# A state-space layer whose output product is moved from VectorE and GpSimd to TensorE transposes, ScalarE and one VectorE sum

## The reference, cut to what matters

```python
dt = softplus(einsum(x_dbl[..., :64], Wdt) + bdt)          # per token and channel
Bm, Cm = x_dbl[..., 64:80], x_dbl[..., 80:96]              # per token and state
dA  = exp(dt[..., None] * A)
dBx = (dt * x)[..., None] * Bm[:, :, None, :]
def step(hc, inp):                                         # over the tokens of a sequence
    dA_t, dBx_t, C_t = inp
    hc = dA_t * hc + dBx_t
    return (hc, einsum('bdn,bn->bd', hc, C_t))
y = (ys + x * Dp) * silu(z);  out = einsum('bld,ed->ble', y, W_out)
```

## Time and profile before

| what | value |
|---|---|
| median of 3 executions | 4015.16 us (4012.3 to 4021.78) |
| profiled execution, device time | 4010.37 us |
| its span, first to last instruction | 4008.4 us |
| mean granted TensorE clock | 0.933 of full speed |
| busy: PE / VectorE (DVE) / ScalarE (ACT) / GpSimd (POOL) | 87% / 68% / 48% / 39% |
| `recur`, first scan to last | 2884.9 to 3811.1 us after the start |

### The profile page before, as it was taken

The page is one execution under the profiler, slowest core; times in us unless marked ns, Lnnn a source line. Parts: engine busy times, 40 slices in busy tenths (PEclk is TensorE's granted clock), DMA queues, the critical chain, the costliest instruction groups (busy, mean ns, idle before and its releaser), DMA issues. The chain is left out here.

```text
span 4008.4 us, 128424 instructions
## 1 busy us (share of the span) xinstructions
PE 3504.0 (87%) x53914; PEld 2508.5 (63%) x53915; DVE 2740.8 (68%) x4691; ACT 1943.7 (48%) x3015; POOL 1561.9 (39%) x1491
## 2 busy tenths in 40 slices
PE   6999999999782899579999999998778788788778
PEld 4888888888671566348888888884232333333257
DVE  5777777777442122257777777776799999999964
ACT  2666666666441122126666666664444444444432
POOL 3333333333132000333333333330278877778900
PEclk8999999999895899879999999999898999999989
DMA  2010010010006100111001001000123222222200
GB/s 68 28 36 28 28 36 28 29 36 12 10 1 263 35 29 31 56 47 36 28 28 36 28 28 36 28 12 25 35 72 85 67 69 71 70 71 78 74 23 21
DMA packets 79949, 182.70 MB, mean 46 GB/s; under 512 B 10754, under 2 KB 31266, under 8 KB 79042
## 3 DMA queue, kind: packets, MB, share of 16 engines
q1 hardware_dynamic: 76354, 166.57, 13.2%
q0 software_dynamic: 3072, 8.39, 0.7%
HBM read 157.36 MB, written 17.56 MB: 44 GB/s over the span
## 5 line engine op out<-in xcount | busy, mean ns | idle before, releaser
L654 ACT ACTIVATE x_probs<-x_score_ps 128x1024 f32<-128x1024 f32 (+1 forms) x896 | 814.2, 961 | 673.8 <-PE x_score_ps L563 667.3
L714 DVE TENSOR_REDUCE x_maxes<-x_misc_ps 128x1 f32<-128x512 f32 (+1 forms) x1792 | 1021.9, 627 | 29.3 <-PE x_misc_ps L481 23.0
L678 POOL CAST x_kT_hi<-x_kT 128x512 fp32r<-128x512 f32 (+1 forms) x448 | 256.9, 574 | 1235.6 <-ACT x_kT L627 1119.5
L1829 POOL TENSOR_TENSOR b_drive<-b_b_all,b_dtx 128x1024 f32<-128x1024 f32 x256 | 602.6, 2355 | 333.4 <-DVE b_dtx L1909 283.3
L1751 PE MATMUL b_acc_ps<-b_read,ident 128*128 128x512 f32 x1024 | 566.9, 684 | 187.9 <-POOL b_read L1837 154.9
L1871 DVE TENSOR_TENSOR_SCAN b_state<-b_decay_ps,b_drive 128x512 f32<-128x512 f32 x512 | 605.1, 1200 | 12.5 <-POOL b_drive L1829 12.5
L557 PE MATMUL x_score_ps<-x_qz,x_kT 32*128 32x128 f32 x13312 | 590.8, 278 | 1.6 <-issue 1.3
L1819 ACT ACTIVATE b_decay_ps<-b_dt,b_a_neg 128x504 f32<-128x504 f32 x512 | 350.0, 685 | 461.7 <-DVE b_state L1871 461.7
L1751 PEld LDWEIGHTS b_acc_ps<-b_read,ident 128*128 128x128 f32 x1024 | 194.8, 212 | 506.3 <-POOL b_read L1837 257.9
L557 PEld LDWEIGHTS x_score_ps<-x_qz,x_kT 32*128 32x128 f32 x13312 | 501.6, 182 | 5.3 <-issue 3.4
L531 PE MATMUL x_misc_ps<-x_probs,x_v 128*32 128x64 f32 x26624 | 464.5, 221 | 0.0
(11 more groups left out here) (283 smaller groups left out, 5583.8 us busy)
## 6 DMA issues: line engine op xcount, KB each, us to landing
x_raw<-in_ctxT SPq DMA_DIRECT2D x64, 800.5 KB, 4.4
b_b_all<-b_bc_rows SPq DMA_DIRECT2D x128, 256.0 KB, 3.6
b_c_all<-b_bc_rows SPq DMA_DIRECT2D x128, 256.0 KB, 3.1
m_w<-in_m_w SPq DMA_DIRECT2D x16, 704.0 KB, 19.3
m_w<-in_m_w SPq DMA_DIRECT2D x8, 768.0 KB, 20.1
m_slot_rows<-m_zero SPq DMA_DIRECT2D x1, 4992.0 KB, 17.2
m_block_rows<-m_slot_rows SPq DMA_DIRECT2D x39, 128.0 KB, 2.0
m_slot_out<-m_out SPq DMA_DIRECT2D x39, 128.0 KB, 1.7
```

Of the source, the lines that this page charges most:

```text
L654: nc.scalar.activation(probs[rows, s % 2, js, 0:n], score_ps[rows, js, 0:n], ACT.Exp).then_inc(exp_done, 1)
L678: nc.gpsimd.tensor_copy(kT_hi[:, at % 3, 0:m * even].rearrange("p (c k) -> p c k", c=m)[:, :, 0:kn], kT[:, b % 2, c:c + m, k0:k0 + kn]).th ...
L714: nc.vector.tensor_reduce(maxes[:, c:c + m, j, k0 // NB], bank(op)[:, 0:m * even].rearrange("p (c k) -> p c k", c=m)[:, :, 0:kn], AX.X, AL ...
L1829: nc.gpsimd.tensor_tensor(drive[:, c:c + 2, :], b_all[:, k % 2:k % 2 + 1, :].broadcast_to([P, 2, NB]), dtx[:, c:c + 2, :], ALU.mult).then_ ...
```

## The change: what it does

The product with C is no longer made with channels on the partitions. Each state is double-buffered in SBUF (`state`, `drive`: two buffers). When all four chunks of a state are scanned, TensorE turns it token tile by token tile (`turn`, four 128x128 transposes per tile of 128 tokens, into one of two PSUM banks). On the turned tile, tokens lie on the partitions, so C is one scalar per partition. C itself is turned once, at the start (`turn_rows`, and one ScalarE copy to `c_turned`). Tiles 0, 2 and 3 are multiplied by ScalarE (`read_tile`) and added to `acc_ps` by TensorE with the product as the stationary operand and the identity as the moving one, which turns them back (`add_up`, four float32 matmuls of 128 columns). Tile 1 is summed over the 16 states by VectorE (`sum_tile`, one instruction per state, behind the next state's first scan), and added once at the end of the pass. `make_c`, `read_chunk`, `read_last`, the high and low parts, and the loads of C per state are gone.

```diff
-            for n in range(NS):
-                k = p * NS + n
-                if n < NS - 1:
-                    make_c(k + 1)
-                for c in range(CI):
-                    gather(k, c)
+        def turn(k, i):
+            if i == 0:
+                pe.wait_ge(state_done, (k + 1) * CI)
+            if i == 0 and k > 0:
+                pe.wait_ge(read_done, (k - 1) * BY_ACT + 2)
+            elif i == 1 and k > 0:
+                pe.wait_ge(read_done, k * BY_ACT)
+            elif i == 2:
+                pe.wait_ge(read_done, k * BY_ACT + 1)
+            elif i == 3:
+                pe.wait_ge(total_done, k + 1)
+            for c in range(CI):
+                ins = nc.tensor.transpose(turn_ps[:, i % 2, c * P:(c + 1) * P], state[:, k % 2, c, i * P:(i + 1) * P],
+                                          ident[:, :])
+            ins.then_inc(turn_done, 1)
+        def add_up(i, part):
+            for c in range(CI):
+                ins = nc.tensor.matmul(acc_ps[:, c, i * P:(i + 1) * P], part[:, c * P:(c + 1) * P], ident[:, :],
+                                       start=False, stop=True, skip_group_check=True)
+            ins.then_inc(acc_done, 1)
+        def gather(k, r):
+            pe.wait_ge(read_done, k * BY_ACT + r + 1)
+            add_up(TILES[r], read[:, r, :])
...
+                turn(k, 0)
+                turn(k, 1)
+                turn(k, 2)
+                gather(k, 0)
+                turn(k, 3)
+                gather(k, 1)
+                gather(k, 2)
+            pe.wait_ge(total_done, (p + 1) * NS)
+            add_up(SUMMED, total)
```

ScalarE, GpSimd and VectorE:

```diff
+        def read_tile(p, n, r):
+            k = p * NS + n
+            i = TILES[r]
+            act.wait_ge(turn_done, k * TPB + i + 1)
+            if k > 0:
+                act.wait_ge(acc_done, p * PARTS + (n - 1) * BY_ACT + r + 1 if n > 0 else p * PARTS)
+            nc.scalar.activation(read[:, r, :], turn_ps[:, i % 2, :], ACT.Copy, scale=c_of(p, n, i)).then_inc(read_done, 1)
...
+                make_decay(p, n, 1)
+                if n > 0:
+                    read_tile(p, n - 1, 0)
+                make_decay(p, n, 2)
+                if n > 0:
+                    read_tile(p, n - 1, 1)
+                    read_tile(p, n - 1, 2)
+                make_decay(p, n, 3)
+                if n < NS - 1:
+                    make_decay(p, n + 1, 0)
...
-        def read_last(k):
-            pool.wait_ge(c_all_in[k % 2], k // 2 * 16 + 16)
-            pool.wait_ge(state_done, k * CI + CI)
-            if k > 0:
-                pool.wait_ge(acc_done, k * CI)
-            nc.gpsimd.tensor_tensor(read[:, VE, :], c_all[:, k % 2, :], state[:, VE, :], ALU.mult).then_inc(pool_read_done, 1)
...
-        def read_chunk(p, n, c):
...
-            nc.vector.tensor_tensor(read[:, c, :], c_ps[:, k % 2, :], state[:, c, :], ALU.mult).then_inc(ve_read_done, 1)
+        def sum_tile(p, n):
...
+            dve.wait_ge(turn_done, k * TPB + SUMMED + 1)
...
+                ins = nc.vector.scalar_tensor_tensor(total[:, :], tile, c_of(p, n, SUMMED), total[:, :], ALU.mult, ALU.add)
+            ins.then_inc(total_done, 1)
...
+                for c in range(CI):
+                    scan(p, n, c)
+                    if c == 0 and n > 0:
+                        sum_tile(p, n - 1)
+            sum_tile(p, NS - 1)
+
+            dve.wait_ge(acc_done, (p + 1) * PARTS)
             for c in range(CI):
-                dve.wait_ge(acc_done, ((p + 1) * NS - 1) * CI + c + 1)
                 nc.vector.tensor_tensor(xc[:, d, c, tokens(p)], acc_ps[:, c, :], zs[:, c, tokens(p)], ALU.mult
                                         ).then_inc(y_done, 1)
```

In `project`, the ScalarE copies of the high parts, VectorE's `low_parts` and two of three row stores per block and direction go:

```diff
-                    nc.scalar.activation(xdbl[:, d, ds(blk * NB, NB)], dbl_ps[:, d, :], ACT.Copy)
-                    act.wait_ge(rows_free, blk * 2 + d + 1)
-                    nc.scalar.activation(hi[R:, d, :], dbl_ps[R:, d, :], ACT.Copy).then_inc(hi_done, 1)
+                    nc.scalar.activation(xdbl[:, d, ds(blk * NB, NB)], dbl_ps[:, d, :], ACT.Copy).then_inc(rows_done, 1)
```

More of the change, by code:

```diff
@@ L1537, in _ @@
                     tokens = ds(blk * NB, NB)
[L1538 to L1543, removed]
+                    sp.wait_ge(rows_done, blk * 2 + d + 3)
+                    sp.dma_start(b_rows[d, :, tokens], xdbl[R:R + NS, d, tokens]).then_inc(rows_out, 16)
+            sp.wait_ge(rows_out, NBLK * 2 * 16)
         @block.tensor
@@ L1672, in recur @@
     b_all = sb("b_b_all", [P, 2, NB])
[L1673 to L1677, removed]
+    c_turned = sb("b_c_turned", [P, 2, NT, NS])
+    drive = sb("b_drive", [P, 2, CI, NB])
+    state = sb("b_state", [P, 2, CI, NB])
+    read = sb("b_read", [P, BY_ACT, DI])
+    total = sb("b_total", [P, DI])
     acc_ps = ps("b_acc_ps", [P, CI, NB])
-    c_ps = ps("b_c_ps", [P, 2, NB])
+    turn_ps = ps("b_turn_ps", [P, 2, NB])
     decay_ps = ps("b_decay_ps", [P, 2, NB])
@@ L1737, in _, with turn_rows @@
         pe.wait_ge(const_done, 1)
[L1739 to L1752, removed]
+        def turn_rows():
+            own = slice(R, R + 2 * NS)
+            for d in range(2):
+                for t in range(NT):
+                    ins = nc.tensor.transpose(turn_ps[:, d, t * 2 * NS:(t + 1) * 2 * NS], xdbl[own, d, t * P:(t + 1) * P],
+                                              ident[own, own])
+            ins.then_inc(rows_turned, 1)
+        def turn(k, i):
[21 more added lines that the diff above has]
+            add_up(TILES[r], read[:, r, :])
         def output(p):
@@ L1772, in _ @@
                 output(p - 1)
+            else:
+                turn_rows()
             for c in range(CI):
@@ L1790, in _, with make_decay @@
     def _(act):
+        def make_decay(p, n, c):
+            q = (p * NS + n) * CI + c
+            if n == 0:
+                act.wait_ge(dt_done, p * CI + c + 1)
+            if q >= 2:
+                act.wait_ge(state_done, q - 1)
+            nc.scalar.activation(by_sequence(decay_ps[:, c % 2, :])[:, :, inside(p)],
+                                 by_sequence(dt[:, c, :])[:, :, inside(p)], ACT.Exp,
+                                 scale=a_neg[:, direction(p)[0], c, n:n + 1]).then_inc(decay_done, 1)
+        def read_tile(p, n, r):
[5 more added lines that the diff above has]
+            nc.scalar.activation(read[:, r, :], turn_ps[:, i % 2, :], ACT.Copy, scale=c_of(p, n, i)).then_inc(read_done, 1)
         nc.scalar.activation(a_neg[:, :, :, :], a_log[:, :, :, :], ACT.Exp).then_inc(a_done, 1)
@@ L1811, in _ @@
             act.wait_ge(edge_done, d + 1)
-            for n in range(NS):
[L1813 to L1820, removed]
-                                         scale=a_neg[:, d, c, n:n + 1]).then_inc(decay_done, 1)
+            if p == 0:
+                act.wait_ge(rows_turned, 1)
+                nc.scalar.activation(c_turned[:, :, :, :],
+                                     turn_ps[:, :, :].rearrange("p d (t r) -> p d t r", r=2 * NS)[:, :, :, NS:], ACT.Copy
+                                     ).then_inc(c_done, 1)
+                act.wait_ge(c_done, 1)
+            for n in range(NS):
+                k = p * NS + n
+                if n == 0:
+                    make_decay(p, 0, 0)
+                make_decay(p, n, 1)
[8 more added lines that the diff above has]
+                    make_decay(p, n + 1, 0)
+            for r in range(BY_ACT):
+                read_tile(p, NS - 1, r)
     @block.gpsimd
@@ L1887, in add_output @@
                 x_t = x_sb[:, t:t + TPH, :].rearrange("p a d -> p (a d)")
-                nc.vector.tensor_tensor(x_t, c_ps[:, i, 0:TPH * D], x_t, ALU.add).then_inc(x_done, 1)
+                nc.vector.tensor_tensor(x_t, turn_ps[:, i, 0:TPH * D], x_t, ALU.add).then_inc(x_done, 1)
         for p in range(PASSES):
```

101 lines of the change are left out of this document (39 added, 62 removed).

## The result

| | before | after |
|---|---|---|
| median | 4015.28 us (4012.3 to 4021.78, 5 runs) | 4034.59 us (4029.2 to 4035.85, 5 runs) |
| profiled execution, device time (span) | 4010.37 (4008.4) | 4031.89 (4030.1) |
| mean granted clock | 0.933 | 0.942 |

The kernel became slower: the ratio is 1.0041, with a 95% interval from 1.0026 to 1.0055, that is 10 to 22 us. Forecast were 4038 us and +23.

The account below looks back on a forecast made before the run. VectorE was taken to bound the kernel before, the chain through PE and ScalarE after. States -10, tail +38 and project -5 give +23 us, added to the median: 4038 us, range 4005 to 4085 us.

Parts of the forecast that it names:

- The chain of a state: In each state, transposes, reads, adding matmuls, ScalarE's last read and decay lead to the scan of chunk 3: 6.12 us.
- Scaled copy: ScalarE's read of a tile from PSUM with a scale per partition takes 0.69 us; 0.606 is the lower bound.
- rival 1: No measurable change: with reads of 0.61 us a state's chain is 5.90 us, 4012 us in all; chance 0.17.
- VectorE's wait: VectorE stands idle about 0.8 us per state before the scan of chunk 3, released by ScalarE's decay.
- First state: A pass's first state, with no products to do, ends its last scan 4.7 us after its first starts.
- Second state: The first transposes of a pass meet half clock, lengthening the chain by 1.7 us, bounds 0 and 4.6.
- States together: Over 8 passes: the states of a pass take 98.2 us against 99.5, -10 us.
- The tail: After a pass's last scan, gating waits for all adding; the next product comes 4.7 us later: +38 us.
- Project: In `project`, eight subtractions go (2.4 us counted) and the last store follows the last row copy (2.4 us): -5 us.
- Rival 3: The clock falls inside the states and PE is the bound: if half of 120 do, +150 us, 4190 us; chance 0.08.
- Rivals 2 and 4: Faster, by one-row products or tile 3's transposes before adding, 3983 us, chance 0.13; slower by longer hand-offs, 4096 us, chance 0.15.
- Rival 4: Hand-offs of 0.85 us and unhidden first weight loads in the chain: 6.6 us, +58, 4096 us; chance 0.15.

Follow-up runs that it names:

- The swaps of ScalarE's and of PE's queue: Changed kernel with chunk 3's decay ahead of the read of tile 3: 3939.98 us; or with tile 3 turned before tile 0 is added: 3935.22 us.
- the decay's swap: Changed kernel, with ScalarE making the decay of chunk 3 before it reads tile 3: 3939.98 us, 0.9813 of before.
- the 50 transposes: Changed kernel, with 50 transposes of the identity on PE in the first state of each pass: 4022.37 us, 1.0019 of before.
- The tail by chunk: Changed kernel, with the last tile and the total added per chunk and each gate waiting for its own chunk alone: 4019.82 us, 1.0011 of before.

## Why the prediction was right

- **The chain of a state,** forecast 6.12 us, measured 6.09: no step is off by more than 0.08. The swaps of ScalarE's and of PE's queue each cut it and took some 95 to 100 us, which shows that this path, not VectorE's or PE's amount of work, set the state.
- **Scaled copy.** The choice of 0.69 and not 0.606 was most of what parted the forecast from rival 1; the read takes 0.688. The chain has two reads: at 0.61 they would have made a state of 5.96 us, 19 us less in all. Rival 1's 5.90 also has the second hand-off at 0.69, and that one took 0.75.
- **VectorE's wait** is there (0.68 before the scan of chunk 3, forecast 0.8), but the view names "issue" and not the decay as its releaser. That the decay ends it is read from the times, 3185.40 + 0.68 = 3186.08 (a decay is 679 ns long) and the scan at 3186.17, and shown by the decay's swap, with which the wait is gone.
- **First state** 4.64 us (forecast 4.7). **Second state** +1.54 (forecast +1.7 of bounds 0 and 4.6); PE had idled 7.36 us before its first transposes, met them at 0.50 (8 weight loads in 1.57 us, at full clock 0.85), and the 50 transposes took the excess away.
- **States together:** -16 us, forecast -10. The term is off by small amounts that all lie on one side: 0.03 us in each of 120 intervals (3.6 us), 0.16 in the excess of 8 second states and 0.06 in 8 first ones (1.8). The 1.7 and its bounds were a choice between values, not a sum, so that 1.54 came so near is in part luck.
- **The tail:** the next product 7.11 us after the last scan, forecast 7.25; +38 us as forecast. The tail by chunk takes 0.85 us from it, with 1.0 expected.
- **Project:** -5.7 us, forecast -5, and both halves of the forecast are there. The last row copy ends 2860.58 - 2750.39 = 110.19 us after the layer's first instruction, against 113.14 before: -2.9 us. From its end to the first scan it is 24.27 against 26.98: -2.7 us. Both were forecast at 2.4. From the first table load of `recur` to the first scan it is 21.25 us against 21.47, so the turning of C costs nothing that can be seen. No run tests this term, and in the traces of the experiments, which don't touch `project`, it comes out at -4.1 to -5.5.
- **Rival 3** (the clock falls inside states) did not happen: 1.00 from 3136.00 to 3222.50. But it was near: with the adding of two tiles gone, it lengthened every one of the 120 intervals, at 4203.7 us where the rival had 4190.
- **Rivals 2 and 4:** no product took one row (24 adding rows a state, x3072); tile 3's transposes came where the program has them; and from transposes to reader it took 0.69 and 0.75 us, not 0.85. Rival 4's own terms (0.16 + 0.10 + 3 x 0.1) make 6.68 us and +67, not 6.6 and +58; nothing hangs on it.
- **How near the number is.** The terms as measured make +16 us where +23 was forecast, the states being 6 us off. The medians differ by 19, and the layers ahead of this one, which the change doesn't touch, start it up to 14 us earlier or later from trace to trace. So the mechanism is what the runs bear out; that 4038 met 4034.59 within 4 us is in part luck.

## What to carry to other kernels

Work taken from the busiest engine pays only as far as the chain that now runs through the others lets it: write the new chain down from the end of the last instruction of one round to the next, engine by engine in queue order, before counting busy time. In it, look for an instruction that the bound engine needs and that stands in a queue behind one that nobody needs yet; two swaps there and the sum moved by one scan turned +0.4% into -2.3%. Bring the clock into the account of an engine off the path: its idle time can slow the chain that runs through it.

## What was not expected of the hardware

- Less work on PE made the kernel 4.2% slower (4203.7 against 4034.59 us), in one execution, since the granted clock of a pass fell from 0.96 to 0.73; eight transposes of nothing in the place of each left-out group gave all of it back.
- Before the change the clock was lower (0.88 of full in a pass) than after (0.96), and no cost of it can be seen there, since VectorE was busy for 99.49 of 99.50 us; after it, 4% below full cost 12 us.
- A wait that a view ends by "issue" (80.5 of the scans' 99.7 us) can still be a wait for another engine: here the decay ends 0.09 us before the scan starts.
